# One chunk of a table product placed behind the first units of the edge stage, and all zero writes of M placed on SyncE

## What is computed

```
h  = relu(layernorm(x))
f  = mish(concat(h[src], h[dst], edge_attr) @ W1 + b1)   # 40000 x 512, W1 is 1088 x 512
m  = mish(f @ W2 + b2)                                   # 40000 x 512
agg = segment_sum(m, dst)                                # 1250 x 512
y  = layernorm(h + mish(concat(h, agg) @ W3 + b3) @ W4 + b4) * gamma + beta
x1 = x + y
x  = x1 + relu(segment_sum((relu(layernorm(x1)) @ U * s @ Vt)[src] * w, dst) + bias)
```

## Time and profile before

| | us |
|---|---|
| median of three runs | 1520.46 |
| the profiled execution | 1521.57 |
| its span in the profile | 1519.9 |
| TensorE busy | 1490.8 (98%) |
| VectorE busy | 1410.4 (93%) |
| ScalarE busy | 1301.2 (86%) |
| GpSimd busy | 1079.2 (71%) |
| mean granted clock of TensorE | 0.996 |

### The profile page before, as it was taken

One profiled execution on the slowest core, in us unless ns is written; L12 is line 12 of the kernel. 1 busy time (PEld: TensorE's weight loads), 2 busy tenths in 40 slices (PEclk: granted clock), 3 DMA queues, 4 the chain that ended last, 5 costly groups with the idle time before them and its releaser, 6 DMA issues.

```text
span 1519.9 us, 33370 instructions
## 1 busy us (share of the span) xinstructions
PE 1490.8 (98%) x7862; PEld 1168.3 (77%) x7862; DVE 1410.4 (93%) x2920; ACT 1301.2 (86%) x2510; POOL 1079.2 (71%) x981
## 2 busy tenths in 40 slices
PE   7979999999999999999999999999999999999998
PEld 6767777777777777777777777777777777777885
DVE  7879999999999999999999999999999999996676
ACT  5079999999999999999999999999999999996562
POOL 1257888888888888877888887888778888863320
PEclk9989999999999999999999999999999999999999
DMA  8874454455555445554554555555455555554773
GB/s 289 293 240 120 115 129 116 116 125 123 121 118 124 116 115 124 121 123 116 127 116 115 125 124 120 117 125 119 115 122 125 120 118 124 117 134 99 177 165 149
DMA packets 123605, 205.10 MB, mean 135 GB/s; under 512 B 31642, under 2 KB 55834, under 8 KB 123569
## 3 DMA queue, kind: packets, MB, share of 16 engines
q0 software_dynamic: 58960, 114.88, 34.7%
q1 hardware_dynamic: 64256, 89.27, 18.9%
q10 hardware_dynamic: 352, 0.52, 0.1%
HBM read 151.60 MB, written 42.75 MB: 128 GB/s over the span
## 4 chain that ended last, share of the span: by engine, by line
PE 81%; issue 5%; DVE 4%; POOL 3%; DMA 3%; ACT 2%; POOLq 1%; SPq 0%; DVEq 0%; ACTq 0%
PE bm L1152 48%; PE bp L1131 6%; PE bp L1139 5%; PE bs L1175 4%; PE bp L1141 4%; PE pm L1163 2%; PE pu L337 2%; PE po L2140 2%; PE pu L2118 2%; PE pB L727 1%; PE pm L1162 1%; DMA xg<-A_tab,idx 1%; POOL M_tab L1082 1%; POOL agg_tab L1071 1%; POOL hTl L1057 1%
## 5 line engine op out<-in xcount | busy, mean ns | idle before, releaser
L1057 POOL TENSOR_TENSOR hTl<-tp,hTh 128x512 fp32r<-128x512 f32 (+1 forms) x314 | 411.3, 1310 | 205.2 <-DVE khl L1351 204.4
L1152 PE MATMUL bm<-W2h,hTh 128*128 128x512 f32 x1252 | 498.5, 398 | 0.9 <-DVE bm L1344 0.5
L1152 PE MATMUL bm<-W2l,hTh 128*128 128x512 f32 x1252 | 497.2, 397 | 0.0
L1152 PE MATMUL bm<-W2h,hTl 128*128 128x512 f32 x1252 | 494.9, 395 | 0.0
L1044 POOL DMA_INDIRECT xg<-A_tab,idx x305 | 319.0, 1046 | 55.0 <-issue 39.3
L1152 PEld LDWEIGHTS bm<-W2h,hTh 128*128 128x128 f32 x1252 | 235.7, 188 | 70.5 <-DVE bm L1344 14.9
L1152 PEld LDWEIGHTS bm<-W2l,hTh 128*128 128x128 f32 x1252 | 235.7, 188 | 57.5
L1211 ACT ACTIVATE rp<-bp 128x512 f32<-128x512 f32 (+1 forms) x314 | 183.2, 584 | 109.8 <-PE bp L1141 80.4
L1152 PEld LDWEIGHTS bm<-W2h,hTl 128*128 128x128 f32 x1252 | 235.9, 188 | 53.7
L1315 DVE SCALAR_TENSOR_TENSOR rp<-rp 128x512 f32<-128x512 f32 (+1 forms) x314 | 214.8, 684 | 38.5 <-ACT rp L1211 25.0
L1325 DVE SCALAR_TENSOR_TENSOR tp<-rp,bp 128x512 f32<-128x512 f32 (+1 forms) x314 | 211.6, 674 | 4.7 <-ACT rp L1217 2.4
(11 more groups left out here) (249 smaller groups left out, 2309.0 us busy)
## 6 DMA issues: line engine op xcount, KB each, us to landing
ea<-in_eaT SPq DMA_DIRECT2D x156, 128.0 KB
M_tab<-mev POOLq DMA_DIRECT2D x157, 80.0 KB, 6.0
agg_tab<-ev POOLq DMA_DIRECT2D x157, 64.0 KB, 2.8
db<-in_dst_rows SPq DMA_DIRECT2D x78, 128.0 KB
M<-M SPq DMA_DIRECT2D x76, 128.0 KB
xg<-A_tab,idx POOLq DMA_INDIRECT x313
eaW<-Bh_tab SPq DMA_DIRECT2D x77, 64.0 KB
eaW<-Bl_tab SPq DMA_DIRECT2D x77, 64.0 KB
```

What stands on the lines that cost most here:

```text
L1057: e.tensor_tensor(hTl[p][:, j, 0:w], pick(u, start_t, tp)[:, 0:w], hTh[p][:, j, 0:w], ALU.subtract)\
L1152: last = e.matmul(bank[0:r, :], a[p][:, c, j * P:j * P + r], w[:, c, :], start=False, stop=c == KC - 1 and w is W2l, skip_group_check=True)
```

## The change

1. B's tenth chunk (c = 9) leaves the prologue of TensorE. It is multiplied behind the products of units 0 to 3. VectorE takes it from its bank behind the first chain's `pre` of unit 3, with the sum in ta[0] and not in tb[0], and SyncE's save_b(9) follows it. GpSimd's `low` of units 1 to 3 waits in addition for the end of B's tenth product.
2. VectorE's bias copies for banks 2 and 3 go from the first chain to its end, behind the tenth chunk's three operations and `square` of unit 4. VectorE's wait for B's stores goes from ahead of slot 0 to ahead of the message of unit 2.
3. The three zero writes of M on GpSimd are gone. SyncE issues all ten: three behind group 2's window rows, two behind group 3's indices, three behind group 3's window rows, two behind group 3's window copy. Group 2's window copy thus has three zero writes ahead of it and not seven.

```diff
-M_EARLY = 3
@@ store_b
-                e.tensor_tensor(tb[i][:], pB[i][:, :], b1b[:], ALU.add).then_inc(c_tb, 1)
+                total = tb[i] if c < NCH - 1 else ta[0]
+                if c == NCH - 1:
+                    a_stored(e)
+                e.tensor_tensor(total[:], pB[i][:, :], b1b[:], ALU.add).then_inc(c_tb, 1)
...
@@ prologue, gpsimd
-                for i in range(M_EARLY):
-                    e.wait_ge(c_B, 2 * i + 6)
-                    zero_m(e, i, q_z)
@@ prologue, tensor
-                for c in range(NCH):
-                    table_b(c)
+                for c in range(NCH - 1):
+                    table_b(e, c)
@@ edge stage, sync
             window_rows(At(None, 8))
-            for i in range(M_EARLY, NCH):
+            for i in range(3):
                 zero_m(e, i, q_zlate)
             window_copy(At(None, 8))
-            loads(At(None, 12))
+            indices(At(None, 12))
+            for i in range(3, 5):
+                zero_m(e, i, q_zlate)
+            features(At(None, 12))
+            targets(At(None, 12))
+            window_rows(At(None, 12))
+            for i in range(5, 8):
+                zero_m(e, i, q_zlate)
+            window_copy(At(None, 12))
+            for i in range(8, NCH):
+                zero_m(e, i, q_zlate)
@@ edge stage, gpsimd, low
                 if first(u) and j:
                     e.wait_ge(a_high, j)
+                    e.wait_ge(c_B, NCH)
@@ edge stage, gpsimd, step
-                            e.wait_ge(q_z, 16 * (ZERO_DMAS + M_EARLY))
-                            e.wait_ge(q_zlate, 16 * (NCH - M_EARLY))
+                            e.wait_ge(q_z, 16 * ZERO_DMAS)
+                            e.wait_ge(q_zlate, 16 * NCH)
@@ edge stage, tensor
-            e.wait_ge(c_tb, 3 * (NCH - 2) + 1)
             for j in range(SUB):
+                if j == SUB - 1:
+                    e.wait_ge(c_tb, 3 * (NCH - 2) + 1)
                 gathered(At(None, j))
             for j in range(SUB):
                 products(At(None, j))
+            table_b(e, NCH - 1)
@@ edge stage, vector, msg
+                if m.reg is None and m.const == 2:
+                    b_stored(e)
@@ edge stage, vector
-            for c in range(NCH):
+            for c in range(NCH - 1):
                 store_b(e, c)
...
-            square(u[0])
-            square(u[1])
-            biases(2)
-            square(u[2])
-            biases(3)
+            for j in range(3):
+                square(u[j])
             pre(u[0], 0)
             pre(u[0], 1)
             square(u[3])
             for j in range(1, SUB):
                 pre(u[j], 0)
+            store_b(e, NCH - 1)
             square(u[4])
-            b_stored(e)
+            biases(2)
+            biases(3)
             slots(e, 0, LOOP0, LOOP1, LAST, step)
```

More of the change, by code:

```diff
@@ L464, in store_b @@
                     e.wait_ge(q_sb[i], 32 * (c // TB))
-                e.tensor_tensor(tb[i][:], pB[i][:, :], b1b[:], ALU.add).then_inc(c_tb, 1)
+                total = tb[i] if c < NCH - 1 else ta[0]
+                if c == NCH - 1:
+                    a_stored(e)
+                e.tensor_tensor(total[:], pB[i][:, :], b1b[:], ALU.add).then_inc(c_tb, 1)
                 e.wait_ge(c_tb, 3 * c + 1)
-                e.tensor_copy(tbh[i][:], tb[i][:]).then_inc(c_tb, 1)
+                e.tensor_copy(tbh[i][:], total[:]).then_inc(c_tb, 1)
                 e.wait_ge(c_tb, 3 * c + 2)
-                e.tensor_tensor(tbl[i][:], tb[i][:], tbh[i][:], ALU.subtract).then_inc(c_tb, 1)
+                e.tensor_tensor(tbl[i][:], total[:], tbh[i][:], ALU.subtract).then_inc(c_tb, 1)
             def evac(e, c):
@@ L710, in _, with table, table_b @@
                 store_a(e, 9)
+            def table(e, c, half, bank):
+                n = 0
+                for a, w in ((nTh, w1h), (nTl, w1h), (nTh, w1l)):
+                    if c == 0 and a is nTh and w is w1h:
+                        e.wait_ge(*((c_w1h, 1) if half else (c_v.sem, v["w1h"])))
+                    if c == 0 and w is w1l:
+                        e.wait_ge(c_v.sem, v["w1l", half])
+                    if half == 0 and a is nTl:
+                        e.wait_ge(c_lo, c + 1)
+                    for k in range(KC):
+                        last = e.matmul(bank[:, :], a[:, k, c * P:(c + 1) * P], w[:, half * KC + k, :],
+                                        start=n == 0, stop=n == 3 * KC - 1)
+                        n += 1
+                return last
+            def table_b(e, c):
+                if c >= TB:
+                    e.wait_ge(c_tb, 3 * (c - TB) + 1)
+                table(e, c, 1, pB[c % TB]).then_inc(c_B, 1)
             @prologue.on("tensor")
@@ L714, in _ @@
                 e.wait_ge(c_g.sem, 4)
[L716 to L730, removed]
                 def table_a(c):
@@ L736, in table_a @@
                         e.wait_ge(c_ta, c - 1)
[L737 to L743, removed]
+                    table(e, c, 0, pA[c % 2]).then_inc(c_A, 1)
                 for c in range(NCH):
@@ L852, in edge_narrow @@
     xg, idx, ea, db, q_in, q_ix, q_ga = (k[n] for n in ("xg", "idx", "ea", "db", "q_in", "q_ix", "q_ga"))
-    b_stored, store_b, save_b, q_b2, c_ta, c_tb = (
-        k[n] for n in ("b_stored", "store_b", "save_b", "q_b2", "c_ta", "c_tb"))
+    b_stored, store_b, save_b, table_b, q_b2, c_ta, c_tb, c_B = (
+        k[n] for n in ("b_stored", "store_b", "save_b", "table_b", "q_b2", "c_ta", "c_tb", "c_B"))
     A_d, Bh_d, Bl_d, agg_d, eaT, src_idx, dst_rows = (k[n] for n in ("A_d", "Bh_d", "Bl_d", "agg_d", "eaT", "src_idx", "dst_rows"))
@@ L1447, in edge_general @@
         k[n] for n in ("q_z", "load_w3", "load_ag", "split_w3x", "xpart", "s_fin", "s_agg"))
-    load_v3, zero_m, settled, store_b, save_b = (
-        k[n] for n in ("load_v3", "zero_m", "settled", "store_b", "save_b"))
+    load_v3, zero_m, settled, store_b, save_b, table_b = (
+        k[n] for n in ("load_v3", "zero_m", "settled", "store_b", "save_b", "table_b"))
     st, sb, ps = scope()
@@ L1581, in _ @@
             e.wait_ge(chain.s, chain.n)
-            e.wait_ge(q_z, 16 * (ZERO_DMAS + M_EARLY))
+            e.wait_ge(q_z, 16 * ZERO_DMAS)
             e.dma_start(agg_d.rearrange("(c p) n -> p c n", p=P), agg[:]).then_inc(q_agg, 16)
             e.wait_ge(q_agg, 16)
-            e.wait_ge(q_zrest, 16 * (NCH - M_EARLY))
+            e.wait_ge(q_zrest, 16 * NCH)
             e.sem_inc(s_out, 1)
@@ L1597, in _ @@
             settled(e)
-            for i in range(M_EARLY, NCH):
+            for i in range(NCH):
                 zero_m(e, i, q_zrest)
```

## The result

The changed kernel is slower: 1525.14 us (median of 10 runs, 1522.70 to 1528.91) against 1520.62 us for the kernel before, timed beside it (10 runs, 1519.80 to 1521.90), a ratio of 1.0029 with a 95% interval of 1.0021 to 1.0038. The forecast was 1515.0. Of all executions for this document, one of the kernel before (2004.48 us) and one of a variant (2341.04 us) ran slow, at mean granted clocks of 0.655 and 0.557, and are left out of every median and ratio.

A forecast was written before the change was run, and what follows sets the result against it. It took TensorE, 81% of the chain that ended last, as the bound through its start of the steady state. 4.2 + 2.4 - 0.5 - 0.6 = 5.5 us off the median 1520.46 gave 1515.0, range 1512.7 to 1519.0.

The forecast's parts named there:

- B's tenth chunk off TensorE's path: Prologue to edge stage: the chunk fills 2.79 us of an idle 3.11; transposes and first product start 2.8 us earlier.
- the two bounds: Group 0's window rows, ahead of unit 0's product: landing no earlier (gain 0), or by 72.1 (gain 2.8 us).
- The bias copies at nothing: First chain: moving two VectorE copies of 0.69 us behind unit 4's square gains nothing and loses nothing.
- VectorE's part: Behind the first chain: the tenth chunk's three operations start at 80.95 and end at 83.75, the middle of 82.85 to 84.65.
- the working with two blockings: VectorE's tenth-chunk operations, blocked twice beside GpSimd's low halves, end at 84.65.
- Group 2's window rows at 87.6: SyncE's queue: tenth store issued at 84.2, landing 3.4 us later; window rows go at 87.6, 6.3 us later than before.
- The copy at 96.2: Slot 3: group 2's window copy lands at 96.2 behind three zero writes; TensorE resumes at 96.3, 4.2 us earlier.
- The clock's 2.4 us: Slot 3: with a stop of 2.7 us the clock stays at 2.4 GHz, giving back 2.4 us.
- Group 3's features: Slot 4: features and targets land at 101.0 behind two more zero writes, holding unit 4's message; loss 0.5 us.
- Group 3's last gather, a loss of 0.6: Slot 7: the gather, wanted at 113.0, lands at about 113.7 behind SyncE's queue; loss 0.7, rounded to 0.6 us.
- The rival that ended slower: Slots 6 and 7: zero writes' backlog delays group 3's last gather and GpSimd's first write to M; 1524.4 us, chance 0.08.

The follow-up runs named there:

- both cures: Changed kernel with five zero writes between B's ninth and tenth store, three behind group 3's target rows, two behind its window copy; 1517.87 us, ratio 0.9982.
- the last variant: Kernel of both cures with unit 4's square ahead of the tenth chunk's operations and one bias copy back in the first chain; 1516.81 us, ratio 0.9976.

## Why the prediction was wrong

It took the right place for the bound and the right resource for the danger, and the sign came out wrong by terms of SyncE's queue. Step by step:

- **B's tenth chunk off TensorE's path: half right.** It costs nothing between the products and unit 4, as said. But unit 0's product started at 73.40 and not at 72.1, after 1.13 us of waiting for the window rows: 1.5 us of the 2.8, between the two bounds. ScalarE began to issue them at 66.61, 1.3 us later than in the earlier trace rows, and the last of them, Bl_tab's of group 0, at 69.78 (69.48 before). The fourth transpose waited 0.75 us for the ninth chunk's sum, where I had some 0.1; the wait for the window rows covered it.
- **The bias copies at nothing: right** as far as the runs tell, 0.9982 against 0.9983.
- **VectorE's part: too short.** The three operations took 3.36 us (82.14 to 85.50), not 2.8, and ended at 85.50, not 83.75; the working with two blockings, 3.7 us from the start, was the better value. 1.2 us of the delay is the late start (82.14 for 80.95). The Trainium skill, in SBUF — State Buffer, section "SBUF: two separate sides", calls the shared port pair an exclusive lock. The trace agrees: the cast and the subtraction took 0.94 and 1.66 us beside GpSimd's low halves, where the kernel before has 0.43 (at 75.01) and 0.69; the sum, which reads PSUM, took 0.68 beside one. In the variant with the zero writes back the cast alone took 2.49 us beside two low halves and the three operations 3.93, so 3.7 is no upper bound.
- **Group 2's window rows at 87.6: wrong, 90.86.** The store is two DMAs, the high half and then the low half, and the window rows wait for both. 1.7 us of the 3.3 come from the issue of the low half (85.89 for 84.2, which stood in the place of 76.56), the other 1.6 from the time behind it: 4.97 us to the window rows, where I had 3.4. I had read that time off, which hold the high half alone; the earlier trace rows had the very interval, 76.56 to 81.34, 4.78 us, and in the kernel before the low half's times to landing are 2.4, 5.3 and 5.9 us (min, median, max). Idle engines were no reason to go below it either: they were idle only up to the issue, and GpSimd's gathers of 85.09 and 86.64 ran beside it. Over the variants the interval was 3.1 to 5.8 us.
- **The copy at 96.2: wrong by that, nearly alone.** From the first zero write to the copy's landing I had 7.7 us, and it took 8.2 (91.74 to about 99.9). The terms for bandwidth were sound. TensorE resumed at 100.00, so 4.2 us of gain became 0.5.
- **The clock's 2.4 us: right in size and place.** In slot 3 it stayed at 1.00, and unit 9's product came 2.92 us early, 2.4 more than unit 8's. What was missed is the stop of 2.04 us in slot 1, which I had put at 0.4; the clock fell there. The waits behind took both up.
- **"Group 3's features": the step that failed.** I had them at 101.0 and a loss of 0.5 us. They landed at 107.4 and cost 6.34 us, 4.54 of waiting and 1.8 of clock. Of the 6.4 us by which they were late, 3.7 came down the queue from the copy. The other 2.7 are an omission. I counted two zero writes and the loads, but the rows show SyncE spending 1.34 us on the indices, 2.05 on the zero writes and 2.70 on the features merely to issue them while the engines were full, so the target rows left at 102.14 only; they landed 4.7 us after that issue, with group 3's window rows and the next zero writes already in flight. The sum of this step has to be taken along the queue, not by bytes. And a second thing was missed: I let the features hold the last third of unit 4's message, but the bias copy for its bank (L1358) stands on VectorE behind the cast, so the message's first matmul waited, which TensorE wants 2.0 us sooner (4.6 us behind unit 8's product, not 6.6); it was released 1.7 us after the landing, where I had 2.3. 0.5 + 2.7 + 2.0 - 0.6 is 4.6, the wait that was measured.
- **Group 3's last gather, a loss of 0.6: right in kind.** It was hidden here by the stop in slot 4 and appeared, as 1.9 to 2.9 us, in each variant that removed that stop and left the zero writes bunched. The rule of the Trainium skill, in DMA: Bandwidth & Descriptors, section "SWDGE vs HWDGE vs iDMA", by which the engines go round in turn between the queues, gives no even shares here: 0.01 MB of 0.73 in 2 us with a gather waiting, 23.8 and 37.4% of the engines' time in the stretches beside. Whether the engines took turns all the same, with few of a gather's descriptors ready at a time, these views do not show.
- **The rival that ended slower** had the backlog of zero writes reaching group 3, but by the gathers and GpSimd's first write to M. It came by VectorE's wait for the target rows, 12 us earlier. I gave it 0.08, with each term ahead of it at a middle value. With the landing and VectorE's end at the bounds that I had set myself, the window rows go 3 us later and the gain of 4.2 is 1.2: no margin for what was left out behind the copy.

The account up to slot 7: 5.5 us forecast, less 3.7 at the copy, less 5.8 at the features (6.34 for 0.5), plus the 0.6 of the gather that stayed hidden, is -3.4, which is what unit 12's transposes show (122.56 for 119.15). The medians have 4.5 us, 1.1 more, which the drift behind slot 7 can hold and which no run takes apart.

By parts, then: the third is worth 2.8 us with the rest as before. The second is worth nothing that can be measured. The first costs 7.1 us on top of the other two (9 with the old zero writes, by 1529.28 against 1520.35), nothing measurable with the zero writes spread.

Open are two things. The changed kernel's runs spread over 6.2 us, those before over 2.1, and only one was profiled. And the clock fell in slot 1 of the changed kernel after a stop of 2.04 us, but not after 2.05 us with both cures and the same TensorE work ahead of it, and again after one of 1.05 us in the last variant; in slot 7 it fell after 1.86 us with the tenth chunk back and stayed after 2.27 us with the bias copies back as well. I can't say what decides. So the forecast's 2.4 us for the clock came true in its place, but the length of a stop alone could not have promised it.

## What to carry to other kernels

Price a moved step by what is queued behind its last DMA on the issuing engine. 9.5 us of delay in one queue outweighed 2.8 us taken off the busiest engine. Place bulk writes where a wait stands anyway (here ahead of a store that everything behind it waits for) and behind every load that is due, never in a block ahead of one; then look at the gathers, which such a block starves without a wait on its own queue. And where three uncertain terms lie in a row on one queue, their bounds add up: the sum at the far ends is a rival of its own, and deserves more than a tail's chance.

## What the runs showed of the hardware

- A store of 256 KB issued onto idle DMA engines (share 0.00 in 84 to 86) let its waiter go 4.97 us after issue, with two gathers beside it; the same store onto full engines in the kernel before took 4.78 (76.56 to 81.34, share 1.03 in 76 to 78). Idle engines at the issue promise nothing.
- SyncE's issues grow when the engines are full: 0.88 us for a zero write at 91.74, 1.03 at 97.30, 1.35 for one transfer of features at 99.40, where the variant with five zero writes in the idle stretch took 0.58 for each transfer of features, at 93.03 (share 0.56 in 92 to 94). The long issue is a delay of its own for what is queued behind.
- A gather beside SyncE's zero writes and loads got 1.4% of the engines' time against 104.5% in one stretch of 2 us, then moved 0.25 MB within one (110 to 111). In four variants TensorE waited 1.9 to 2.9 us for such a gather.
- Two kernels with the same TensorE work and stops of 2.04 and 2.05 us ahead of slot 1 had different clocks behind it, 0.50 in 90 to 92 and 1.00.
